# State-space phase of a Mamba and MoE kernel: one 1024-column scan per state, and step-times-B of nine of the sixteen states formed on ScalarE in time-major layout and transposed by TensorE

## What is computed

```python
u, z = split(x @ Win.T)                      # 256 inner channels each
u = silu(conv4(u) + convb)                   # along time
dtr, Bm, Cm = split(u @ Wx.T)                # 8, 16 and 16 columns
dt = softplus(dtr @ Wdt.T + bdt)             # [512, 256]
A = -exp(Alog)                               # [256, 16]
def step(h, t):                              # h: [256, 16]
    h = exp(dt[t][:, None] * A) * h + (dt[t] * u[t])[:, None] * Bm[t][None, :]
    return h, h @ Cm[t]
y = scan(step) + u * D
out = (y * silu(z)) @ Wout.T                 # [512, 128]
```

## Time and profile before

| | us |
|---|---|
| median of 3 runs (2261.31 to 2267.13) | 2262.24 |
| span of the profiled execution | 2259.9 |
| state-space phase in it, from the first `dt` to the last `yg` | 42.3 to 1048.4 |
| attention and experts | 1066 to 2260 |

### The profile page before, as it was taken

How to read it: one execution, slowest core, us unless ns; L and a number is a source line. 1 busy time by engine, 2 the same in 40 slices (tenths; PEclk the granted TensorE clock), 3 DMA queues, 4 the chain that set the end, 5 groups by cost and what they waited for, 6 DMA issues and landing times.

```text
span 2259.9 us, 29525 instructions
## 1 busy us (share of the span) xinstructions
PE 1616.6 (72%) x7664; PEld 944.2 (42%) x7664; DVE 1664.1 (74%) x2666; ACT 1176.0 (52%) x1906; POOL 1242.9 (55%) x1129
## 2 busy tenths in 40 slices
PE   3677676757777675765376887787878878787887
PEld 1455444545455454543133343443434434343443
DVE  3999999999999999996252638456384663847455
...
DMA packets 39646, 107.44 MB, mean 48 GB/s; under 512 B 4128, under 2 KB 30048, under 8 KB 34368
## 3 DMA queue, kind: packets, MB, share of 16 engines
...
## 4 chain that ended last, share of the span: by engine, by line
issue 25%; POOL 13%; PE 6%; DVE 4%; DMA 2%; ACT 1%; SPq 0%; POOLq 0%; DVEq 0%; ACTq 0%
POOL pp L1891 9%; DMA k<-k_scratch 1%; DVE mx L1589 1%; PE pbk L1220 1%; PE pa L1214 1%; PE po L1227 1%; PE og L1163 1%; PE scores L1115 1%; POOL rt L1821 1%; PE scores L1113 1%; DVE rec L1617 0%; POOL kp L1854 0%; DVE stats L1532 0%; ACT pt L1410 0%; POOL rotk L1850 0%
## 5 line engine op out<-in xcount | busy, mean ns | idle before, releaser
L725 POOL TENSOR_TENSOR hc<-hb,cb 128x512 f32<-128x512 f32 x512 | 654.0, 1294 | 262.2 <-DVE hb L612 229.9
L612 DVE TENSOR_TENSOR_SCAN hb<-da,dbu 128x512 f32<-128x512 f32 x512 | 600.4, 1201 | 4.6 <-DVE stats L576 3.1
L497 ACT ACTIVATE da<-dt,a_neg 128x512 f32<-128x512 f32 x512 | 351.8, 717 | 348.2 <-DVE hb L612 298.3
L329 PE MATMUL yp<-ident,hc 128*128 128x128 f32 x2048 | 366.1, 322 | 62.0 <-POOL hc L725 61.5
L1891 POOL TENSOR_TENSOR pp<-pt,pp 128x512 f16<-128x512 f32 x320 | 365.2, 1152 | 74.2 <-ACT pt L1410 73.7
L329 PEld LDWEIGHTS yp<-ident,hc 128*128 128x128 f32 x2048 | 304.0, 168 | 172.6 <-POOL hc L725 91.4
L605 DVE TENSOR_TENSOR dbu<-dtu,bp 128x512 f32<-128x512 f32 x512 | 323.4, 675 | 3.4 <-PE bp L317 2.2
L1589 DVE TENSOR_REDUCE mx<-scores 128x1 f32<-128x384 f32 (+3 forms) x352 | 218.5, 636 | 126.9 <-PE scores L1115 124.0
L1699 DVE SCALAR_TENSOR_TENSOR ga<-th,pa 128x512 f32<-128x512 f32 x128 | 87.6, 685 | 231.5 <-ACT th L1425 231.5
L1409 ACT ACTIVATE pp<-scores,lift 128x512 f16<-128x512 f32 x320 | 221.9, 693 | 63.9 <-PE scores L1143 63.2
L317 PE MATMUL bp<-st,sel 96*128 96x512 bf16 x256 | 118.5, 463 | 152.9 <-DVE dbu L605 150.0
...
## 6 DMA issues: line engine op xcount, KB each, us to landing
...
cb<-c_scratch SPq DMA_DIRECT2D x16, 1024.0 KB, 4.7
...
```

The source lines that it names most:

```text
L329: last = nc.tensor.matmul(yp[:, c, h * P:(h + 1) * P], src[:, c * P:(c + 1) * P], ident[:, :], is_transpose=True, start=(s < 0 and h == 0 ...
L497: nc.scalar.activation(da[:, s % NDA, :], dt[:, d, h, :], ACT.Exp, scale=a_neg[:, d, h, n:n + 1]).then_inc(da_done, 1)
L612: nc.vector.tensor_tensor_scan(hb[:, s % NHB, :], da[:, s % NDA, :], dbu[:, s % 2, :], 0.0, ALU.mult, ALU.add).then_inc(scan_done, 1)
L725: nc.gpsimd.tensor_tensor(hc[:, s % NHC, :], hb[:, s % NHB, :], cb[:, d, s // 2, :], ALU.mult).then_inc(hc_done, 1)
```

## The change

A step is now a whole state of both halves. `da`, `hb`, `hc` and `dbu` are 1024 columns wide (2 x 512); column 0 of each half of `da` is set to zero once and never written again, so that one scan runs over both halves. `hb`, `hc` and `da` have 4 buffers of a state, `dbu` 2 (4 PSUM banks); `bp` and `ud` are gone. `cb` is one buffer, loaded in four groups of four states.

For the seven states in `BY_DVE` TensorE writes the spread B twice, straight into `dbu` (`pe_fill`), and VectorE multiplies in place. For the nine in `BY_ACT` ScalarE multiplies in a time-major layout: once per unit TensorE transposes `xd` (`pe_xdt`, to get B with time on the partitions; ScalarE copies it, `act_bt`) and `dtu` (`pe_dtut`; copied by `act_dtut`); then for each such state ScalarE makes four products of 128x256 with B as the scale of a partition (`act_dbut`), and TensorE transposes them in eight 128x128 pieces into `dbu` (`pe_fill`). A fill of state `n` waits for the scan of state `n-2`. `u * D` becomes a matmul with a diagonal matrix (`diag_d`). The order of the work in a unit is written anew: TensorE issues `pe_u` at steps 14 to 19 (16 to 21 for `d = 0`), `pe_z` at 22, `pe_xd` at 23, `pe_dt` at 25 and 26, `pe_xdt` at 29; ScalarE the silus at step 23, `act_xd` at 24 and 26, softplus at 27 and 28, `act_bt` at 29; VectorE `dt` and `dtu` both ahead of the last scan.

```diff
+BY_ACT = (3, 4, 6, 7, 9, 10, 12, 13, 15)
+BY_DVE = tuple(n for n in range(NS) if n not in BY_ACT)
+NA, ND = len(BY_ACT), len(BY_DVE)
+NGROUP = 4
+PER_GROUP = NS // NGROUP
+LAG_N = 2
...
+        diag_d = sb("diag_d", [P, NDIR, NH2, P])
+        dtut = sb("dtut", [P, NDIR, TC, DI])
+        bt = sb("bt", [P, NDIR, TC, NS])
+        cb = sb("cb", [P, NS, SEQ])
...
-        NDA, NHB, NHC = 8, 4, 8
-        da = sb("da", [P, NDA, SEQ])
-        sel32 = da[0:SPLIT_ROWS, 0:NS * P // SEQ, :].rearrange("r a (n p) -> r (a n) p", p=P)
-        hb = sb("hb", [P, NHB, SEQ])
-        hc = sb("hc", [P, NHC, SEQ])
-        bp = pb("bp", [P, 2, SEQ])
-        dbu = pb("dbu", [P, 2, SEQ])
+        NDA, NHB, NHC, NTB = 4, 4, 4, 3
+        da = sb("da", [P, NDA, NH2, SEQ])
+        hb = sb("hb", [P, NHB, NH2 * SEQ])
+        hc = sb("hc", [P, NHC, NH2, SEQ])
+        dbut = sb("dbut", [P, NTB, TC, DI])
+        sel32 = dbut[0:SPLIT_ROWS, 0:2].rearrange("r a c n -> r (a c n)").rearrange("r (n p) -> r n p", p=P)
+        dbu = pb("dbu", [P, 2, NH2, SEQ])
...
+        def sp_c_load(sp, b, d, g):
             written = count.in_register(sp, c_written, b, 16 * d + 16)
-            hc_before = count.in_register(sp, hc_done, b, STEPS * (d - 1))
+            used = count.in_register(sp, hc_done, b, NS * (d - 1) + PER_GROUP * (g + 1))
             sp.wait_ge(c_written, written)
-            sp.wait_ge(hc_done, hc_before)
-            sp.dma_start(cb[:, d, 0:C_FIRST], cscr[d:d + 1, 0:C_FIRST].to_broadcast([P, C_FIRST, SEQ])
-                         ).then_inc(c_first, 16)
-            sp.dma_start(cb[:, d, C_FIRST:], cscr[d:d + 1, C_FIRST:].to_broadcast([P, NS - C_FIRST, SEQ])
-                         ).then_inc(c_rest, 16)
+            sp.wait_ge(hc_done, used)
+            n0, n1 = PER_GROUP * g, PER_GROUP * (g + 1)
+            sp.dma_start(cb[:, n0:n1], cscr[d:d + 1, n0:n1].to_broadcast([P, PER_GROUP, SEQ])
+                         ).then_inc(c_group[g], 16)
...
+        def pe_fill(pe, b, d, n):
+            pe.wait_ge(scan_done, count(scan_done, b, NS * d + n - 1))
+            if n in BY_DVE:
+                if n == 0:
+                    pe.wait_ge(part_done, count(part_done, b, d + 1))
+                    pe.wait_ge(xd_done, count(xd_done, b, 4 * d + 3))
+                for h in range(NH2):
+                    last = nc.tensor.matmul(dbu[:, n % 2, h, :], sel[:, n, :], st[:, d, :], start=True, stop=True)
+            else:
+                pe.wait_ge(dbut_done, count(dbut_done, b, NA * d + BY_ACT.index(n) + 1))
+                for h in range(NH2):
+                    for c in range(TC):
+                        last = nc.tensor.transpose(dbu[:, n % 2, h, c * P:(c + 1) * P],
+                                                   dbut[:, BY_ACT.index(n) % NTB, c, h * P:(h + 1) * P], ident[:, :])
+            last.then_inc(b_ready, 1)
+        def pe_xdt(pe, b, d):
+            pe.wait_ge(soft_done, count(soft_done, b, 8 * d + 2))
+            for c in range(TC):
+                last = nc.tensor.transpose(wp[:, 1 - d, c * P:(c + 1) * P], xd[:, c * P:(c + 1) * P], ident[:, :])
+            last.then_inc(xdt_ready, 1)
+        def pe_dtut(pe, b, d):
+            pe.wait_ge(bt_done, count(bt_done, b, d + 1))
+            pe.wait_ge(soft_done, count(soft_done, b, 8 * d + 6))
+            pe.wait_ge(dt_done, count(dt_done, b, 2 * d + 2))
+            for c in range(TC):
+                for h in range(NH2):
+                    at = c % 2 * DI + h * P
+                    last = nc.tensor.transpose(wp[:, c // 2, at:at + P], dtu[:, d, h, c * P:(c + 1) * P], ident[:, :])
+            last.then_inc(dtut_ready, 1)
...
+            if n < 0:
+                pe.wait_ge(diag_set, NDIR * NH2)
                 pe.wait_ge(yg_done, count(yg_done, b, d))
-            else:
-                pe.wait_ge(hc_done, count(hc_done, b, STEPS * d + s + 1))
-            for h in (range(NH2) if s < 0 else (s % 2,)):
-                src = ud[:, h, :] if s < 0 else hc[:, s % NHC, :]
-                for c in range(TC):
-                    last = nc.tensor.matmul(yp[:, c, h * P:(h + 1) * P], src[:, c * P:(c + 1) * P], ident[:, :],
-                                            is_transpose=True, start=(s < 0 and h == 0 and c % 2 == 0),
-                                            stop=(s == STEPS - 1), skip_group_check=True)
+                for h in range(NH2):
+                    for c in range(TC):
+                        last = nc.tensor.matmul(yp[:, c, h * P:(h + 1) * P], u[:, h, c * P:(c + 1) * P],
+                                                diag_d[:, d, h, :], start=(h == 0 and c % 2 == 0), stop=False,
+                                                skip_group_check=True)
...
+        def pe_front(pe, b, d, s):
+            if s == 13 and d == 0:
+                pe_xt(pe, b)
+            for i in range(NH2 * NTAP):
+                if s == (14, 15, 15, 16, 17, 18, 18, 19)[i] + 2 * (d == 0):
+                    pe_u(pe, b, d, i)
+            if s == 22:
+                pe_z(pe, b, d, 0)
+                pe_z(pe, b, d, 1)
+            if s == 23:
+                pe_xd(pe, b, d)
+            if s in (25, 26):
+                pe_dt(pe, b, d, s - 25)
+            if s == 29:
+                pe_xdt(pe, b, d)
...
+                n = s // 2
+                if s % 2 == 0:
+                    if n + 1 < NS:
+                        pe_fill(pe, b, d, n + 1)
+                    elif after:
+                        pe_fill(pe, *after, 0)
+                else:
+                    if n < LAG_N and tail:
+                        pe_y(pe, *tail, NS - LAG_N + n)
+                    if n == LAG_N + 1:
+                        for m in range(-1, n - LAG_N):
+                            pe_y(pe, b, d, m)
+                    if n > LAG_N:
+                        pe_y(pe, b, d, n - LAG_N)
+                if s == 1:
+                    pe_dtut(pe, b, d)
+                if tail and s == 8:
                     pe_ygt(pe, *tail)
-                if tail and tail[1] == 1 and s in (10, 11, 12, 13):
-                    pe_out(pe, tail[0], s - 10)
+                if tail and tail[1] == 1 and s in (13, 14):
+                    pe_out(pe, tail[0], 2 * (s - 13))
+                    pe_out(pe, tail[0], 2 * (s - 13) + 1)
...
-        def act_ud(act, b, d, h):
-            if h == 0:
-                act.wait_ge(y_added, count(y_added, b, y_count(d - 1, 0)))
-            nc.scalar.activation(ud[:, h, :], u[:, h, :], ACT.Copy, scale=col[:, d, h, 2:3]).then_inc(ud_done, 1)
+        def act_bt(act, b, d):
+            act.wait_ge(xdt_ready, count(xdt_ready, b, d + 1))
+            nc.scalar.activation(bt[:, d], wp[:, 1 - d, :].rearrange("p (c r) -> p c r", c=TC)[:, :, 0:NS],
+                                 ACT.Copy).then_inc(bt_done, 1)
+        def act_dtut(act, b, d):
+            act.wait_ge(dtut_ready, count(dtut_ready, b, d + 1))
+            act.wait_ge(dbut_done, count(dbut_done, b, NA * (d - 1)))
+            nc.scalar.activation(dtut[:, d].rearrange("p c n -> p (c n)"), wp[:, :, :].rearrange("p k n -> p (k n)"),
+                                 ACT.Copy).then_inc(dtut_done, 1)
+        def act_dbut(act, b, d, n):
+            k = BY_ACT.index(n)
+            if k == 0:
+                act.wait_ge(dtut_done, count(dtut_done, b, d + 1))
+            slot_before = BY_ACT[k - NTB] + (NS * d if k >= NTB else NS * (d - 1))
+            act.wait_ge(b_ready, count(b_ready, b, slot_before + 1))
+            for c in range(TC):
+                last = nc.scalar.activation(dbut[:, k % NTB, c, :], dtut[:, d, c, :], ACT.Copy,
+                                            scale=bt[:, d, c, n:n + 1])
+            last.then_inc(dbut_done, 1)
         def act_da(act, b, d, s):
             n, h = s // 2, s % 2
             if s == 0:
                 act.wait_ge(dt_done, count(dt_done, b, 2 * d + 1))
-            act.wait_ge(scan_done, count(scan_done, b, STEPS * d + s + 1 - NDA))
-            nc.scalar.activation(da[:, s % NDA, :], dt[:, d, h, :], ACT.Exp,
+            if h == 0:
+                act.wait_ge(scan_done, count(scan_done, b, NS * d + n + 1 - NDA))
+            nc.scalar.activation(da[:, n % NDA, h, 1:], dt[:, d, h, 1:], ACT.Exp,
...
+        def act_front(act, b, d, at):
+            if at == 17 and d == 0:
                 act_xpad(act, b, 0)
...
                 act_xpad(act, b, 1)
...
+            if at == 23:
                 act_silu_u(act, b, d, 0)
                 act_silu_u(act, b, d, 1)
                 act_silu_z(act, b, d, 0)
                 act_silu_z(act, b, d, 1)
                 act.preload_act_table_set("natural_log_exp_and_others")
...
+            if at == 24:
+                act_xd(act, b, d, 0)
+                act_xd(act, b, d, 1)
+            if at == 26:
+                act_xd(act, b, d, 2)
+                act_xd(act, b, d, 3)
+            if at in (27, 28):
+                for k in range(4):
```

(51 more changed lines are left out.)

197 lines of the change are left out of this document (75 added, 122 removed).

## The result

The changed kernel takes 2386.4 us in the median of 4 runs (2385.7 to 2388.5), the kernel before 2262.9 beside it: a ratio of 1.0547 (1.0527 to 1.0567). That is slower, as forecast, but by 124 us where 84 was said, and 1.4 us above the range's upper end.

A forecast was written before the change was run, and what follows sets the result against it. VectorE's queue was taken to bound the state-space phase; 9.6 us saved a unit against later scans gave +59 us, the clock +25: 2262 + 84 = 2346 us, range 2205 to 2385, likeliest 2300 to 2385.

The forecast's parts named there:

- the saving: VectorE's scans and products in the state-space phase: 9.6 us a unit saved, 152 over the phase, if nobody else is late.
- the sum: All units' gains and losses together +59 us, clock +25, giving 2262 + 84 = 2346 us.
- unit B: A unit of the state-space phase with a `d = 0` front, 65.1 us from `dt` to `dt` before the change.
- A: A unit of the state-space phase with a `d = 1` front, 61.6 us from `dt` to `dt` before the change.
- clock term: TensorE at half clock after idling before fills 13 and 15: one of the two groups late, 1.65 us a unit.
- The walk from `pe_u` to scan 12: Silus wait for the later `pe_u`, so `da` of state 12 is late: 7.05 us lost in unit B, 8.5 in A.
- The stretch from scan 12 on: ScalarE's queue, waiting for TensorE, delays scans 13 to 15: 5.8 us lost in unit B, 4.5 in A.
- the durations of VectorE's own work: From scan 12 to the unit's end VectorE's own work, with `dt` and `dtu`, was put at 12.8 us; `x1t` at 1.3.
- (1): Rival: VectorE stays the bound, a unit's losses stay under 9.6 us, and the kernel gets faster; chance 0.23.
- (3): Clock rival: all TensorE groups late, 2371 us, or none, 2321; counted within the forecast's chance of 0.58.
- (4): Rival: transposes never bring TensorE's full clock, 2542 us; counted within the 0.06 for above 2385.
- The reading that no drain follows the table load: ScalarE's table switches carry no added 1.38 us drain; with it the sum would be some 1.4 us a unit higher.

The follow-up runs named there:

- e9: The changed kernel with the front's silus, `xd` copies, softplus, `bt`, `pe_z`, `pe_xd` and `pe_dt` one state later; 2350.4 us.
- e12: The changed kernel with six states by ScalarE, GpSimd's product 14 held behind `dtu`, `pe_xdt` at step 27, and TensorE's front earlier; 2295.4 us.
- e4: The changed kernel with unread spread matmuls on TensorE, 12 ahead of the fill of state 13 and 20 ahead of that of 15; 2367.2 us.
- e5: The changed kernel with GpSimd's product of state 14 held back until `dtu` is written; 2391.0 us.
- e13: e6 with GpSimd's products of states 2 and 5 held back until `xln` and `xn` are written, in units with a `d = 0` front; 2325.8 us.
- e2: The changed kernel with the transpose of `xd` (`pe_xdt`) at step 27 in place of 29, ahead of the fill of state 15; 2386.8 us.
- e6: The changed kernel with GpSimd's product of state 14 held back until `dtu` is written and `pe_xdt` at step 27; 2359.1 us.

## Why the prediction was right and where it was wrong

*What bounds it, and which way it goes: right.* The prices behind the saving are as stated: 3.63 us for a state of VectorE's (249.97 to 253.60), 2.20 for one of ScalarE's. (54.6 - 45.1 is 9.5, not 9.6, some 1.5 us in the sum.) VectorE's busy time from `dt` to `dt` is 57.2 in unit B, not 63. The kernel is slower because 15 fronts lose more than 9.6 us each.

*Where the 34 us lie.* The sum gave B 4.9 us more than before with its clock term, and A 7.05. Measured are 9.1 and 7.7. So seven units of B make 29 of the 34 us by which the phase was missed.

*The walk from `pe_u` to scan 12: right.* 7.05 us was given for B, 6.74 stands in the trace; the wait of `res` and its queue in A is there too, 9.3 us from scan 9 to scan 12 where 8.5 was given. Scan 13 waits 1.84 (1.9 in the walk). Narrow products of ScalarE: 1.6 us for four. Cause shown by e9 and e12: both put more steps between `pe_u` and the silus, and the wait before scan 12 goes.

*The stretch from scan 12 on: a size off, by the clock term.* In B scan 14 waits 4.45, the walk had 3.1. ScalarE waited 2.14 us for `pe_dt` where the walk had 0.4, because fill 13 and what follows ran at half clock. Of the **clock term** one group in two was taken, 1.65 us. In B both groups came late, in A only the second. e4 gets 22.4 us back from them, 1.5 a unit in the mean, close to the 1.65; but the second group's lateness doesn't show in it, since `dtu` holds scan 15 up as long.

*The step that failed: the durations of VectorE's own work.* `dtu`, `xln`, `xn` and `x1t` were entered with what they took before, and of GpSimd's doubled product it was only asked whether it is hidden in GpSimd's own queue. These four and GpSimd's products hold each other off for a whole instruction, and one of these products now lasts 2.4 us and runs beside each of them: `dtu` 1.19 to 3.17, `x1t` 1.34 to 3.18, `xln` 1.28 to 2.35, `xn` 2.14 to 3.20. e5 and e13 take it away at three of the places and find 1.23, 1.10 and 1.09 us; `x1t` of the last batch, with nothing of GpSimd's beside it, takes 1.12 in both kernels. The scans and products, with an operand in PSUM, don't show it (2.28 and 1.21 to 1.22 in all runs), nor do the statistics (`BATCH_NORM_STATS2`, one input in SBUF: 0.86 before, 0.85 beside a product of 2.37).

What it cost, in B: `xln` and `xn` lie where VectorE has no slack, 2.1 us. Scan 15 starts 7.66 us behind scan 14 where the walk had 5.6, so 2.1 more. That is `dtu`; but the `da` of 15 is late by the same 2 us, since the fill of 15, `yp` and `pe_xdt` ahead of `bt` took 4.6 us at half clock where the walk had 2.5. e2 and e5 take one of the two away and gain next to nothing; e6 takes both away, and B is 3.6 us shorter. With 1.5 for scan 14, less 0.3 at scan 12 and the 1.65 already taken, this makes 3.8 of the 4.2 us. In A scan 15 is 1.8 late as well, and the long `x1t` just fills the wait that the walk left there; against them stands the clock term, whose first group ran at full clock. That these nearly cancel in A is luck. e6 and e13 together give 62.7 us, more than the miss: they contain the clock's share in A, and `xn` in e13 is shorter than it was in the kernel before.

The Trainium skill, "SBUF — State Buffer", section on the two separate sides, states this: VectorE and GpSimd share a pair of ports that one of them holds for the whole instruction when VectorE has two SBUF inputs or a two-port mode. The trace agrees: `dtu` ends 1.1 us, about its own length, after GpSimd's product, and that product takes 0.8 us more beside the last 0.96 us of `dt`.

*The rivals.* (1) fails: losses are 17 to 19 us a unit, not under 9.6. (3), all groups late and 2371, holds in B alone, and 2371 would leave 9 of the 118 us. (4) fails: the clock averages 0.85 in the phase. The reading that no drain follows the table load holds here too: 300.54 + 1.28 is 301.82, and `da` starts at 301.83. The range's upper end was missed by 1.4 us, less than the 7.2 that the second phase gave.

*Outside the forecast:* 7.2 us of the second phase.
